# Two orders changed in an LSTM step: which wait a VectorE instruction carries, and where three matmuls stand in TensorE's queue

## The reference

```
xn = layernorm(x)
x  = x + gnn(xn, src, dst) + mix(xn)        # edge sums, MLP, batch norm; linear attention with an MLP
x  = x + ffn(layernorm(x))
```

```
def step(carry, xp):                         # xp = x_t @ W_ih.T + biases, 1024 gates
    h, c = carry
    gates = xp + h @ W_hh.T
    i, f, g, o = split(gates, 4)
    c = sigmoid(f) * c + sigmoid(i) * tanh(g)
    h = sigmoid(o) * tanh(c)
    return (h, c), h
```

## Time and profile before

| what | us |
|---|---|
| median of 3 runs | 15350.32 |
| lowest, highest | 15345.05, 15354.82 |
| the profiled execution | 15353.04 |
| its span, first to last instruction | 15350.2 |
| TensorE busy | 9953.5 |
| VectorE busy | 10365.1 |
| ScalarE busy | 4955.5 |
| weight loads on TensorE, busy | 9025.8 |

### The profile page before, as it was taken

The page is one execution under the profiler, slowest core; times in us unless marked ns, Lnnn a source line. Parts: engine busy times, 40 slices in busy tenths (PEclk is TensorE's granted clock), DMA queues, the critical chain, the costliest instruction groups (busy, mean ns, idle before and its releaser), DMA issues. The chain is left out here.

```text
span 15350.2 us, 691245 instructions
## 1 busy us (share of the span) xinstructions
PE 9953.5 (65%) x255269; PEld 9025.8 (59%) x255269; DVE 10365.1 (68%) x84126; ACT 4955.5 (32%) x32393; POOL 2065.8 (13%) x1598
## 2 busy tenths in 40 slices
PE   3444444866666666666666666666666666666666
PEld 2333333766666666666666666666666666666665
DVE  4443222577777777777777777777777777777777
ACT  1111111333333333333333333333333333333333
POOL 5887887000000000000000000000000000000000
PEclk7666777755555555555555555555555555555556
DMA  6555555100000000000000000000000000000000
GB/s 159 89 91 85 83 83 85 59 1 1 1 1 1 1 1 1 1 1 1 1 1 1 1 1 1 1 1 1 1 1 1 1 1 1 1 1 1 1 1 17
DMA packets 617504, 301.47 MB, mean 20 GB/s; under 512 B 454943, under 2 KB 573747, under 8 KB 616843
## 3 DMA queue, kind: packets, MB, share of 16 engines
q0 software_dynamic: 150048, 204.90, 8.3%
q1 hardware_dynamic: 456678, 91.09, 3.3%
q10 hardware_dynamic: 10742, 5.06, 0.1%
HBM read 153.07 MB, written 141.27 MB: 19 GB/s over the span
## 5 line engine op out<-in xcount | busy, mean ns | idle before, releaser
L1416 PE MATMUL bank<-hp,whh 128*128 128x1 f16 (+1 forms) x200000 | 7030.9, 168 | 3793.6 <-DVE hp L1547 3793.6
L1416 PEld LDWEIGHTS bank<-hp,whh 128*128 128x128 f16 x200000 | 6519.5, 106 | 4336.8 <-DVE hp L1547 4336.0
L1481 ACT ACTIVATE gates<-bank 128x4 f32<-128x4 f32 x12500 | 2183.1, 175 | 7435.9 <-DVE bank L1519 7045.8
L1519 DVE TENSOR_REDUCE bank<-bank 128x4 f32<-128x8 f32 x12500 | 2171.4, 174 | 2666.9 <-PE bank L1416 2260.9
L1547 DVE TENSOR_TENSOR hp<-bank,sg 128x1 f16<-128x1 f32 x12500 | 2004.3, 162 | 409.3
L1490 ACT ACTIVATE bank<-gates 128x1 f32<-128x1 f32 x12500 | 2067.5, 165 | 324.3
L1552 DVE SCALAR_TENSOR_TENSOR hp<-bank,sg,hp 128x1 f16<-128x1 f32 x12500 | 2164.2, 216 | 0.0
L1416 PE MATMUL bank<-xsteps,wih 128*128 128x10 f16 (+1 forms) x40032 | 2163.9, 170 | 0.0
L1527 DVE CUSTOM_DVE_ANT_1 uv<-gates 128x4 f32<-128x4 f32 x12500 | 1994.8, 160 | 2.2
L1416 PEld LDWEIGHTS bank<-xsteps,wih 128*128 128x128 f16 x40032 | 1750.5, 104 | 0.0
L1626 POOL TENSOR_TENSOR U<-U (+1 forms) x25 | 27.6, 1140 | 12541.0 <-POOLq L1569 12541.0
(11 more groups left out here) (179 smaller groups left out, 3499.1 us busy)
## 6 DMA issues: line engine op xcount, KB each, us to landing
xsteps<-x_d SPq DMA_DIRECT2D x1252, 5.0 KB, 1.7
U<-hp SPq DMA_DIRECT2D x1250, 5.0 KB, 1.7
acc_d<-zero SPq DMA_DIRECT2D x30, 640.0 KB, 12.6
ht<-acc_d SPq DMA_DIRECT2D x75, 224.0 KB
rows<-xn_d,staged_i POOLq DMA_INDIRECT x782, 2.8
acc_d<-sums,target POOLq DMA_INDIRECT x782, 3.8
xi<-xn_d SPq DMA_DIRECT2D x50, 125.0 KB
xi<-in_x SPq DMA_DIRECT2D x50, 125.0 KB
```

Of the source, the lines that this page charges most:

```text
L1416: return nc.tensor.matmul(to, w, v, start=start, stop=True, skip_group_check=True)
L1481: nc.scalar.activation(gates[:, k, 0:2 * NG_[k]:2], zi[k], ACT.Tanh, scale=down)\
L1519: nc.vector.tensor_reduce(zi[k], gi[k][b][:, s], axis=AX.X, op=ALU.add).then_inc(ifg_summed[k], 1)
```

## The change

Two things are reordered, nothing is added or removed. In TensorE's `body`, `gates_of(1, 1, 1)`, three matmuls that need only the first part of half 1 of the state, moves from after `gates_of(1, 0, 0)` to after `gates_of(0, 1, 1)`, ahead of the wait for the second part of half 0. Every product that takes a first part alone then stands ahead of all that take a second one, but for the o gate's. In VectorE's `state1`, the wait for `tc_ready` (the cell's tanh) now stands before the wait for `sg_ready`, so that the product carries the wait for the tanh and the one for sg is the separate instruction.

```diff
@@ -1448,12 +1448,12 @@
                     gates_of(1, 0, 1)
                     pe.wait_ge(h1_ready[1], t + 1)
                     gates_of(0, 1, 1)
+                    gates_of(1, 1, 1)
                     pe.wait_ge(h2_ready[0], t + 1)
                     gates_of(0, 0, 0)
                     pe.wait_ge(h2_ready[1], t + 1)
                     gates_of(0, 1, 0).then_inc(ifg_made[0], 1)
                     gates_of(1, 0, 0)
-                    gates_of(1, 1, 1)
                     gates_of(1, 1, 0).then_inc(ifg_made[1], 1)
@@ -1540,8 +1540,8 @@
                     def state1(k):
+                        dve.wait_ge(tc_ready[k], t + 1)
                         dve.wait_ge(sg_ready[k], t + 1)
-                        dve.wait_ge(tc_ready[k], t + 1)
                         if s == 0 and due(16 * i):
                             dve.wait_ge(h_out[b], 16 * i)
```

## The result

The changed kernel takes 14,675.1 us (14,668.8 to 14,681.4, 4 runs) against 15,351.3: ratio 0.956, interval 0.9543 to 0.9577. That is 676 us faster. The forecast was 14,545, a gain of 806; the time lies in the range of 8 in 10 and near the upper end of the likeliest case's own range, 14,440 to 14,700.

What follows compares the result with a forecast made beforehand. The chain of k = 1 was taken to bind, k = 0 afterwards. Terms -0.04, 0, -0.03 and -0.067 took 1.950 to 1.812 us, plus 0.009 once-in-ten: 1.821, time 14,545; 8-in-10 range 14,440 to 14,980.

Steps and rivals of the forecast that it cites:

- likeliest case: The prediction's own forecast of 14,545 us, given 62%, with its own range 14,440 to 14,700.
- What binds: Loop through product 1, second parts, TensorE's waits, gate sum 1, cell 1 and tanh sets the 1.950 us step.
- two odd places: Once-in-ten late product 0 followed by a shorter step; first ten steps, second part 0 earlier, take 1.91 us.
- The carried wait: VectorE's product 0 behind its cell tanh: start distance falls from 0.10 to 0.035 us, -0.067 a step.
- The three matmuls: TensorE: last matmul before gate sum 0 becomes the 22nd, 0.58 us after the first instead of 0.62, -0.04.
- The distance of the two products: VectorE: product 1 comes 0.18 us after the new product 0, so k = 1 no longer binds.
- Cell tanh 0: ScalarE: o tanh moves 0.12 us earlier, so the cell tanh starts when the accumulator read has ended, -0.03.
- Once in ten: First step of a block: product 0 some 0.09 us late at the store's wait, now paid, 0.009 a step.
- Rival 1: VectorE finishes one instruction before the next, cell 1 stays 0.149 behind sg: gain 390, time 14,960; 15%.
- Rival 2: TensorE's three later waits are held or cost 0.02 us each even when satisfied: gain 434, time 14,916; 12%.
- Rival 3: Lone wait for sg costs what the lone tanh wait did, only the order counts: time 14,960; 5%.
- Rival 4: Moved matmuls delay ready second parts on TensorE, each step 0.036 us longer: +225, time 15,575; 4%.

Runs made afterwards that it cites:

- lowering the counts: Kernel before, state semaphore counts lowered by one, removing the register instruction between product 1 and second part 0: 15,122.8 us; same edit on the changed kernel: 14,664.7.
- wait-only: Changed kernel with the matmul order put back as before, leaving only the swapped waits of state1: 14,881.8 us, ratio 0.969.
- late-o: Changed kernel with two projection matmuls put ahead of the o gate's, so o's sum, tanh and sg of k = 1 come later: 14,700.3 us, ratio 0.957.
- order-only: Changed kernel with the waits of state1 put back as before, leaving only the three moved matmuls: 15,085.4 us, ratio 0.982.
- the two store-wait kernels: Changed kernel, the store's wait moved from the product to a semaphore instruction: ahead of gate sum 0, 14,642.0 us; between the gate sums, 14,640.9.

## Why the prediction was right

**What binds.** Right. No engine fills the stage: VectorE, the busiest, is busy for 0.75 of it before and 0.78 after, so a chain sets the time. That k = 1 bound before was argued from two odd places; lowering the counts, worth 238 us before and next to nothing after, shows it for the part of the chain that runs through the second parts.

**The carried wait.** Right: the records show the two waits exchanged, and 0.10 became 0.032, forecast 0.035. The lone wait for sg costs nothing on this path: it lets product 0 start 0.08 behind sg at the earliest (wait-only and late-o kernels). The upper end of the forecast's own range, 14,700, stood for product 0 held 0.13 behind sg. It is 0.13 behind, and the time is near that end, but by coincidence: sg does not hold it.

**The three matmuls.** Right to the rounding: 22 matmuls without a gap, M0 0.58 after the first. All three later waits were satisfied in time, and by more than the prediction had (two by 0.01, one by 0.03). A held weight load starts 0.053 after the end of the VectorE instruction that releases it, at all three waits before; after the change the three start 0.087, 0.115 and 0.096 after that end, which leaves 0.03, 0.06 and 0.04 to spare.

**The distance of the two products.** Forecast 0.18, measured 0.157. Product 1 came where it was expected, 1.99 after the product 0 of the step before (1.833 + 0.157); product 0 came 0.02 later than expected, for the reason that follows, and that is also why the waits had more to spare.

**Cell tanh 0.** This is the term that was mis-sized. The sum took -0.03 because the tanh no longer stands behind the o tanh: it starts 0.118 after the accumulator read and not 0.145. It does. But it then lasts longer. One cell tanh, before and after:

```profile
8003.59 0.16 ACT L1490 ACTIVATE bank<-gates 128x1 f32<-128x1 f32 x1
```
```profile
8004.00 0.17 ACT L1490 ACTIVATE bank<-gates 128x1 f32<-128x1 f32 x1
```

Over all of them, ns least/median/most, before (half of them short) and after (none):

```profile
L1490 ACT ACTIVATE bank<-gates x12500: 156/166/175, 2997.1 to 15185.4; 128x1 f32<-128x1 f32 x199
```
```profile
L1490 ACT ACTIVATE bank<-gates x12500: 174/174/175, 3002.3 to 14514.5; 128x1 f32<-128x1 f32 x199
```

So the term is -0.028 + 0.018 = -0.01 and not -0.03. The sum becomes -0.04 - 0.01 - 0.069 = -0.119: a common step of 1.83 us, not 1.81. The 0.02 x 6250 = 125 us are nearly all of the 130 that were missing.

**Once in ten.** Right: 1.93 is not followed by a shorter step, 0.009 us a step on average. Taking the wait away gave back 33 of 59 us, because the register and semaphore work moved with it.

**The rivals.** Rival 1 (one VectorE instruction after the other) is out: cell 1 starts 0.07 behind sg, which lasts 0.15. Rival 2 is out by the 24 matmuls in 0.80 us. Rival 3, that the order alone would count, is out: product 0 starts 0.03 behind its tanh, and the order alone gives 15,085. (Its 14,960 was too low, again for the tanh's length, 0.02 a step.) Rival 4 is out: M0 comes 0.04 earlier, not later, and with the order alone the kernel is faster.

## What to carry to other kernels

When two chains share engines in a loop, look for the iterations that are odd for some outside reason: whether their delay is given back in the next iteration tells which chain binds and how much the other can spare. Where an instruction has two waits, read from the trace which of them it carries, and let it be the one that is satisfied last: in these products it was the first in the code, and the hand-over from the tanh went from 0.101 to 0.032 us. Look whether a register instruction stands between the two: once in ten steps here it took over the wait, and the product came 0.09 later. When a stall behind another instruction of the same engine goes away, count what the end gains and not what the start gains: here 0.010 us and not 0.028.

## What the runs showed of the hardware

- In the 10,004 products with two waits, before as after, the product carried the first in the code and the second was a separate instruction of 0.021 us. In the 624 steps with a register instruction behind these two, that one carried the first (after the change at 8013.377, 0.045 long) and product 0 started 0.09 after its start.
- Two instructions here lasted shorter where they started later after the end of what they wait for. The cell tanh lasts 0.156 us where it starts 0.063 after the read it waits for (before; 0.059 to 0.063 wait-only), and 0.174 where it starts 0.033 to 0.036 after it (after, order-only; 0.171 with the late o gate). It is not the distance to the o tanh, which is 0.11 in the late-o kernel as before. Of 0.028 earlier start 0.010 arrived. The new cell of k = 0 on VectorE lasts 0.156 where it starts 0.039 after its gate tanh (before) and 0.164 where it starts 0.032 after it (after).
- Weight loads whose wait was satisfied before their turn cost TensorE nothing here: three such waits stand in the changed kernel's 24 matmuls, which start every 0.027 us from the second on. Before the change, a held wait stretched the interval behind it to some 0.04 to 0.05 us.
- The register instruction between product 1 and second part 0 was worth 0.037 us a step before the change. The same instruction was worth 0.003 a step (1.842 to 1.840) where no binding chain runs through it.
- With the separate wait for sg between them, product 0 started no less than 0.08 us behind the sg instruction in front of it (wait-only, late-o); 0.11 where it waits for two semaphores, the store's too.
- Register and semaphore work in front of a gate sum made it 0.046 us late ahead of the first sum and 0.066 ahead of the second (the two store-wait kernels).
